# A pre-norm attention and low-rank-expert kernel: another order of loads and matmuls in its prologue

## The reference

```
n = layernorm(x); q, k, v = split(n @ Wqkv.T + bqkv)      # 16 heads of 64
scores = q k^T * 64**-0.5 + q . rel_k[clip(i - j, -64, 64)]
scores below the 32nd largest of their row -> -inf; attn = softmax(scores)
v1 = attn v + attn . rel_v[clip(i - j)];  v2 = attn v1;  v3 = attn v2
x = x + (sum_i sigmoid(alpha_i) v_i) @ Wout.T + bout
x = x + layernorm(x) @ base_w.T + base_b + 2 * (8 experts of rank 8, gated by a softmax)
```

## Time and profile before

| what | value |
|---|---|
| median of 3 runs | 720.5 us (716.99 to 725.43) |
| the profiled execution | 719.82 us, its span 718.1 us |
| mean granted clock of TensorE | 0.982 |
| VectorE busy | 684.0 us (95%) |
| TensorE busy | 658.3 us (92%), weight loads 513.4 us |
| ScalarE busy | 620.5 us (86%) |
| GpSimd busy | 533.5 us (74%) |
| start of the first search | 19.79 us |

### The profile page before, as it was taken

How to read it: one execution, slowest core, us unless ns; L and a number is a source line. 1 busy time by engine, 2 the same in 40 slices (tenths; PEclk the granted TensorE clock), 3 DMA queues, 4 the chain that set the end, 5 groups by cost and what they waited for, 6 DMA issues and landing times.

```text
span 718.1 us, 20880 instructions
## 1 busy us (share of the span) xinstructions
PE 658.3 (92%) x5768; PEld 513.4 (72%) x5768; DVE 684.0 (95%) x2841; ACT 620.5 (86%) x1754; POOL 533.5 (74%) x934
## 2 busy tenths in 40 slices
PE   4378999999999999999999999999999999998795
PEld 3266777777777777777777777777777777776574
DVE  6899999999999999999999999999999999999925
ACT  4588999989999899989999899989999899988833
POOL 1588898778777777877787778777878787877411
PEclk9779999999999999999999999999999999999998
DMA  6735455444544455444545454545454445454202
GB/s 204 189 106 160 128 152 154 144 149 141 151 137 148 138 147 150 136 141 144 150 134 151 133 149 137 154 130 149 137 158 140 138 134 160 129 149 116 63 13 58
DMA packets 148338, 98.72 MB, mean 137 GB/s; under 512 B 10624, under 2 KB 147968, under 8 KB 148096
## 3 DMA queue, kind: packets, MB, share of 16 engines
q1 hardware_dynamic: 147920, 97.32, 46.4%
q10 hardware_dynamic: 304, 0.08, 0.1%
HBM read 45.59 MB, written 51.77 MB: 136 GB/s over the span
## 4 chain that ended last, share of the span: by engine, by line
DVE 79%; issue 9%; PE 6%; POOL 2%; DMA 2%; ACT 1%; SPq 0%; DVEq 0%; ACTq 0%; POOLq 0%
DVE top L666 40%; DVE work L672 35%; DMA band_scratch<-zeros 1%; POOL s_sb L322 1%; DVE rinv L653 1%; PE ps_p L885 1%; PE ps_y L902 1%; PE ps_d L871 1%; PE ps_s L965 1%; ACT a_sb L435 1%; DVE stats L688 0%; PE ps_a L800 0%; DMA band_scratch<-band 0%; DMA skew<-band_scratch 0%; DVE x_sb L681 0%
## 5 line engine op out<-in xcount | busy, mean ns | idle before, releaser
L666 DVE MAX8 top<-work 128x8 f32<-128x256 f32 x768 | 285.0, 414 | 0.0
L672 DVE MATCH_REPLACE8 work<-top,work 128x256 f32<-128x256 f32 x512 | 206.1, 411 | 0.0
L322 POOL TENSOR_TENSOR s_sb<-s_sb,pen 128x512 f32<-128x512 f32 x127 | 162.1, 1276 | 55.0 <-ACT pen L425 54.6
L327 POOL TENSOR_SCALAR a_sb<-a_sb,rinv 128x256 f32<-128x256 f32 x254 | 119.6, 482 | 54.6 <-DVE rinv L653 53.7
L435 ACT ACTIVATE a_sb<-s_sb,nmax 128x256 f32<-128x256 f32 x256 | 128.1, 501 | 34.1 <-POOL s_sb L322 26.2
L425 ACT ACTIVATE pen<-s_sb,limit 128x256 f32<-128x256 f32 x254 | 116.5, 512 | 21.7 <-POOL limit L309 21.7
L297 POOL TENSOR_TENSOR s_sb<-s_sb,skew 128x384 f32<-128x384 f32 x128 | 128.6, 1004 | 3.0 <-DMA skew<-band_scratch 3.0
L885 PE MATMUL ps_p<-aT,rows 128*64 128x256 f32 x1024 | 125.1, 385 | 0.9 <-issue 0.5
L672 DVE MATCH_REPLACE8 work<-top,s_sb 128x256 f32<-128x256 f32 x256 | 103.0, 411 | 0.0
L666 DVE MAX8 top<-s_sb 128x8 f32<-128x256 f32 x256 | 94.5, 411 | 3.5 <-POOL s_sb L297 3.5
L885 PEld LDWEIGHTS ps_p<-aT,rows 128*64 128x64 f32 x1024 | 69.0, 136 | 38.5 <-issue 11.9
(11 more groups left out here) (136 smaller groups left out, 1289.9 us busy)
## 6 DMA issues: line engine op xcount, KB each, us to landing
skew<-band_scratch SPq DMA_DIRECT2D x128, 192.0 KB, 2.8
diag_scratch<-a_sb SPq DMA_DIRECT2D x128, 192.0 KB, 2.2
band_scratch<-band SPq DMA_DIRECT2D x128, 191.0 KB, 3.3
diag<-diag_scratch SPq DMA_DIRECT2D x128, 128.0 KB, 2.2
wqkv<-in_wqkv SPq DMA_DIRECT2D x1, 1152.0 KB, 7.7
x_sb<-in_x SPq DMA_DIRECT2D x4, 256.0 KB, 4.9
wout<-in_wout SPq DMA_DIRECT2D x1, 512.0 KB, 5.7
out<-xn SPq DMA_DIRECT2D x1, 512.0 KB, 3.3
```

The lines of the kernel that those rows point to most:

```text
L322: nc.gpsimd.tensor_tensor(s_sb[g % 4][:], s_sb[g % 4][:], pen[g % 2][:], ALU.subtract).then_inc(pen_added, 1)
L327: nc.gpsimd.tensor_scalar(a_sb[g % 3][:, t, :], a_sb[g % 3][:, t, :], rinv[g % 2][:, t:t + 1], 1.0, ALU.mult, ALU.mult).then_inc(normed, 1)
L666: nc.vector.max(m[:, t, 8 * n:8 * n + 8], src).then_inc(top_step, 1)
L672: nc.vector.match_replace(work[t][:, n % 2, :], m[:, t, 8 * n:8 * n + 8], src, LOW).then_inc(top_step, 1)
```

## The change

x is loaded in five groups, the first two of two tiles each, so that the first sequence stands alone; all statistics, roots, transposes and copies follow these groups (XGROUPS), and the fifth group is transposed at the end of slot 3. TensorE runs 12 products of the ones tile with itself into ps_d before anything else. After q/k(0) and relative(0) come scores(0), then q/k(1), relative(1), q/k(2), and ScalarE saves in the same order, with the second root behind save_scores(0). Pair 0's band is filled and sent head by head (fill_first). SP waits for two of POOL's preparations instead of all, and issues the weights of pairs 2 to 7 after both heads' bands of pair 0.

```diff
--- before.py
+++ after.py
@@ -131,7 +131,7 @@
         ps_z = [ps_qk, ps_a, ps_d]
         ps_l = [ps_s0, ps_s1, ps_qk, ps_a, ps_p0, ps_p1]
 
-        x_in = [sem(f"x_in{g}") for g in range(TILES // 4)]
+        x_in = [sem(f"x_in{g}") for g in range(TILES // 4 + 1)]
         relk_in, cols_in, w_in, w_in2, late_in, wout_in, ffn_in = (
             sem(n) for n in ("relk_in", "cols_in", "w_in", "w_in2", "late_in", "wout_in", "ffn_in"))
         made, scratch_zero = sem("made"), sem("scratch_zero")
@@ -185,17 +185,15 @@
         SLOTS = range(-3, PAIRS + 4)
         MADE = 1 + 1 + 1 + 4 + 1 + 1 + 1
         DONE = TILES - T
-        GROUPS = TILES // 4
+        XGROUPS = [(0, T), (T, 4)] + [(a, a + 4) for a in range(4, TILES, 4)]
 
         @block.sync
         def _(sp):
-            for g in range(GROUPS):
-                sp.dma_start(x_sb[:, 4 * g:4 * g + 4, :], x_d[2 * g:2 * g + 2].rearrange("b (t p) d -> p (b t) d", p=P)
-                             ).then_inc(x_in[g], 16)
+            for g, (a, e) in enumerate(XGROUPS):
+                sp.dma_start(x_sb[:, a:e, :], x_d[a // T:e // T].rearrange("b (t p) d -> p (b t) d", p=P)).then_inc(x_in[g], 16)
                 if g == 0:
                     sp.dma_start(wqkv[:, 0:2, :], wqkv_d[:, 0:2 * 3 * P].rearrange("p (h c) -> p h c", h=2)).then_inc(w_in, 16)
-            sp.dma_start(wqkv[:, 2:NP, :], wqkv_d[:, 2 * 3 * P:].rearrange("p (h c) -> p h c", h=NP - 2)).then_inc(w_in2, 16)
-            sp.wait_ge(made, MADE)
+            sp.wait_ge(made, 2)
             for i in range(2):
                 dst = bass.AP(band_d[i].tensor, DYN, [[2 * ROW, P], [ROW, 2], [1, P]])
                 sp.dma_start(dst, zeros[:, 0:2 * P].rearrange("p (h c) -> p h c", h=2)).then_inc(scratch_zero, 16)
@@ -251,7 +249,7 @@
                 if on(q + 2):
                     p = q + 2
                     for h in range(2):
-                        sp.wait_ge(band_filled, p + 1)
+                        sp.wait_ge(band_filled, p + 2 if p else h + 1)
                         ring(sp, skew_in, 2 * p + h - 4)
                         dst = bass.AP(band_d[p % 2].tensor, h * ROW, [[2 * ROW, P], [DYN + P, T], [1, DYN]])
                         sp.dma_start(dst, band[p % 2][:, h, :].rearrange("p (t c) -> p t c", t=T)
@@ -262,6 +260,9 @@
 
             for q in SLOTS:
                 slot(q)
+                if q == -2:
+                    sp.dma_start(wqkv[:, 2:NP, :], wqkv_d[:, 2 * 3 * P:].rearrange("p (h c) -> p h c", h=NP - 2)
+                                 ).then_inc(w_in2, 16)
                 if q == -1:
                     load_wout()
                 if q == 2:
@@ -309,6 +310,13 @@
                 nc.gpsimd.tensor_scalar(limit[g % 2][:], top8[g % 2][:, :, TOPK - 1], STEEP, 1.0, ALU.mult,
                                         ALU.mult).then_inc(limit_done, 1)
 
+            def fill_first(h):
+
+                pool.wait_ge(band_saved, h + 1)
+                edges = bass.AP(band[0][:].tensor, h * T * DYN + FILL, [[2 * T * DYN, P], [2 * P - 1, 2], [0, FILL]])
+                beyond = bass.AP(band[0][:].tensor, h * T * DYN, [[2 * T * DYN, P], [FILL + 2 * P, 2], [1, FILL]])
+                nc.gpsimd.tensor_scalar(beyond, edges, 1.0, 1.0, ALU.mult, ALU.mult).then_inc(band_filled, 1)
+
             def fill_band(p):
 
 
@@ -352,7 +360,10 @@
                     negative_max(2 * q)
                 if on(q - 1):
                     add_penalty(2 * q - 1)
-                if on(q + 2):
+                if q == -2:
+                    fill_first(0)
+                    fill_first(1)
+                elif on(q + 2):
                     fill_band(q + 2)
                 if on(q):
                     add_skew(2 * q + 1)
@@ -405,11 +416,12 @@
                                         (bqkv[:], bqkv_d.rearrange("p (h c) -> p h c", h=NP), cols_in)):
                 act.dma_start(dst, src).then_inc(semaphore, 16)
             act.wait_ge(var_done, 1)
-            nc.scalar.activation(std[:, 0:4], mv[:, 0:4, 1], ACT.Sqrt).then_inc(std_done, 1)
+            nc.scalar.activation(std[:, 0:T], mv[:, 0:T, 1], ACT.Sqrt).then_inc(std_done, 1)
 
             def save_xnT(g):
                 act.wait_ge(xnT_ready, g + 1)
-                nc.scalar.copy(xnT[:, g * 4 * P:(g + 1) * 4 * P], ps_y[:]).then_inc(xnT_saved, 1)
+                a, e = XGROUPS[g]
+                nc.scalar.copy(xnT[:, a * P:e * P], ps_y[:, 0:(e - a) * P]).then_inc(xnT_saved, 1)
 
             def save_aT(g):
                 p = g // 2
@@ -549,19 +561,19 @@
             save_xnT(0)
             act.wait_ge(cols_done, 1)
             save_queries(0)
+            save_band(0)
+            save_scores(0)
             act.wait_ge(var_done, 2)
-            nc.scalar.activation(std[:, 4:TILES], mv[:, 4:TILES, 1], ACT.Sqrt).then_inc(std_done, 1)
-            for q in (-2, -1):
-                save_band(q + 2)
-                if on(q + 1):
-                    save_scores(q + 1)
-                save_queries(q + 3)
+            nc.scalar.activation(std[:, T:TILES], mv[:, T:TILES, 1], ACT.Sqrt).then_inc(std_done, 1)
+            save_queries(1)
+            save_band(1)
+            save_queries(2)
             act.wait_ge(late_in, 16 * 8)
             nc.scalar.activation(al[:], al[:], ACT.Exp, scale=-1.0).then_inc(alpha_exp, 1)
             act.wait_ge(relv_done, 2 * T + 1)
             for q in range(0, PAIRS):
                 slot(q)
-                if 0 <= q < GROUPS - 1:
+                if 0 <= q < len(XGROUPS) - 1:
                     save_xnT(q + 1)
                 if q == PAIRS - 2:
                     act.wait_ge(y_stats, 1)
@@ -613,8 +625,9 @@
 
             def moments(a, e):
                 for i in range(a, e):
-                    if i % 4 == 0:
-                        dve.wait_ge(x_in[i // 4], 16)
+                    for g, (first, _) in enumerate(XGROUPS):
+                        if i == first:
+                            dve.wait_ge(x_in[g], 16)
                     nc.vector.bn_stats(stats[:, i, :], x_sb[:, i, :]).then_inc(row_stats, 1)
                 for i in range(a, e):
                     dve.wait_ge(row_stats, a + i + 1)
@@ -628,17 +641,17 @@
                     nc.vector.tensor_scalar(xn[:, i, :], x_sb[:, i, :], mv[:, i, 0:1], rstd[:, i:i + 1],
                                             ALU.subtract, ALU.mult).then_inc(xn_done, 1)
 
-            moments(0, 4)
+            moments(0, T)
             dve.wait_ge(std_done, 1)
-            normal_rows(0, 4)
+            normal_rows(0, T)
             dve.wait_ge(relk_in, 32)
             own(nc.vector.tensor_scalar(relkt[:, 0, :], relk[:, 0:P], relk[:, P:VOCAB], None, ALU.subtract))
             nc.vector.tensor_scalar(relkt[:, 1, :], relk[:, 1:VOCAB], relk[:, 0:1], None, ALU.subtract).then_inc(relk_done, 1)
             dve.wait_ge(cols_in, 16)
             nc.vector.tensor_scalar(kcol[:], bqkv[:, :, 1], SCALE, None, ALU.mult).then_inc(cols_done, 1)
-            moments(4, TILES)
+            moments(T, TILES)
             dve.wait_ge(std_done, 2)
-            normal_rows(4, TILES)
+            normal_rows(T, TILES)
             dve.wait_ge(late_in, 16 * 8)
             for t in range(T):
                 nc.vector.tensor_scalar(rcol[:, :, t], bqkv[:, :, 2], relvc[:, t:t + 1], None, ALU.add).then_inc(relv_done, 1)
@@ -786,10 +799,11 @@
             mm, transpose = nc.tensor.matmul, nc.tensor.transpose
 
             def normal_columns(g):
-                pe.wait_ge(xn_done, 4 * (g + 1))
+                a, e = XGROUPS[g]
+                pe.wait_ge(xn_done, e)
                 reach(pe, xnT_saved, g)
-                for i in range(4):
-                    last = transpose(ps_y[:, i * P:(i + 1) * P], xn[:, 4 * g + i, :], ident[:])
+                for i in range(a, e):
+                    last = transpose(ps_y[:, (i - a) * P:(i - a + 1) * P], xn[:, i, :], ident[:])
                 last.then_inc(xnT_ready, 1)
 
             def attention_columns(g):
@@ -803,7 +817,7 @@
 
             def queries_and_keys(p):
                 b, hp = divmod(p, NP)
-                pe.wait_ge(xnT_saved, b // 2 + 1)
+                pe.wait_ge(xnT_saved, [g for g, (a, e) in enumerate(XGROUPS) if a <= T * b][-1] + 1)
                 if p == 0:
                     pe.wait_ge(w_in, 16)
                 ps_k = ps_a[:, 0:N] if p == 0 else ps_qk[:, N:2 * N]
@@ -982,18 +996,21 @@
                         if b == e - 1:
                             last.then_inc(l_ready, 1)
 
+            pe.wait_ge(made, 1)
+            for i in range(12):
+                mm(ps_d[:, 0:P], ones[:], ones[:], start=True, stop=True)
             pe.wait_ge(made, MADE)
             normal_columns(0)
             queries_and_keys(0)
-            for q in (-2, -1):
-                relative_keys(q + 2)
-                if on(q + 1):
-                    scores(q + 1)
-                queries_and_keys(q + 3)
+            relative_keys(0)
+            scores(0)
+            queries_and_keys(1)
```

(4 more changed lines are left out.)

## The result

The changed kernel takes 722.15 us (median of 22 runs, 719.13 to 727.42), the kernel before 718.76 us (22 runs beside it, 716.03 to 725.43). The ratio is 1.0048, 95% interval 1.0032 to 1.0064: slower by half a per cent, 3.4 us, where 1.1 us of gain was forecast. The profiled execution has a span of 722.3 us against 718.1.

A forecast was written before the change was run, and what follows sets the result against it. VectorE's 128 top-32 searches, end to end, bound the kernel. An earlier first search (1.4 us) less later slots (0.3) gave 1.1 us; 719.0 us was put between 718.7 (from the profiled execution) and 719.4 (from the median); range 715.8 to 723.3.

The forecast's parts named there:

- rival C: Ramp: weights arrive late for pair 2, delaying the second search through add_skew(1); 720.4 to 723.3 us; chance 0.30.
- C's upper case: Weights land at 19.7, first search 1.5 us late, second 3.2 us late at the slow clock.
- Two tiles first, warm TensorE, band ready: Prologue: two tiles first save 1.5 us, warm-up 0.2, filling by halves 0.3; band ready at 11.1 instead of 13.12.
- The zero fill: SyncE's queue: without the weights in front, the scratch's zeros land 2.8 us earlier, at 10.9 instead of 13.66.
- When the band lands: Pair 0's bands land 2.55 us (first head) and 3.0 us (second head) after the band leaves.
- T: Time the first band leaves: latest of 10.14, 10.9 and 11.1, about 11.0 instead of 13.68.
- When the weights land: Load behind pair 0's bands: its bytes need 2.8 us, so it lands at 16.8.
- The skew read behind the weights: Pair 0's skew read waits for the weights, lands at 17.3; first search at 18.4, gain 1.4 us.
- The work behind the weights: Chain queries(2) to add_skew(1), 6.74 us: ends at 23.5, just before the second search at 23.8, if TensorE is fast.
- point of decision: Weights' landing from which the second search comes later than before: 18.45 at the fast clock, 16.45 at the slow one.
- the slow clock: TensorE idling before the weights land may fall to 1.2 GHz, adding 2.0 us to pair 2's chain; left open.
- The fifth group in slot 3: Four transposes and a copy in slot 3, where TensorE has no gap: cost 0 to 0.55 us, taken 0.3.

The follow-up runs named there:

- e4: The changed kernel without the 12 products of ones at its start; 720.49 us, ratio 1.0037 to the kernel before.
- e9: The changed kernel with the eight small loads issued by GpSimd, on another queue than SyncE's; 721.83 us, ratio 1.0031 to the kernel before.
- e10: e6 with small loads on GpSimd's queue, wout and second scratch's zero fills in slot 0, 12 more products behind queries(2); 719.07 us, ratio 1.0.
- e6: The changed kernel with weights of pairs 2 and 3 before the zero fills, pairs 4 to 7 behind pair 0's skew reads; 718.38 us, ratio 1.0002.
- e2: The kernel before with only the weights of pairs 2 to 7 moved, issued after both bands of pair 0; 723.29 us, ratio 1.0062.
- e5: The changed kernel with the weights of pairs 2 to 7 issued after pair 0's two skew reads; 726.6 us, ratio 1.0115 to the kernel before.
- e16: The changed kernel with x in four groups again; 722.07 us, ratio 1.0042 to the kernel before.
- e3: The changed kernel with 28 more products of ones between relative(1) and queries(2); 719.79 us, ratio 1.0021 to the kernel before.
- e14: The kernel before with only x in five groups, two tiles first, the fifth transposed at the end of slot 3; 718.59 us, ratio 0.9996.
- e1: The changed kernel with the weights of pairs 2 to 7 back behind the x loads, before the zero fills; 720.04 us, ratio 1.002 to the kernel before.
- e7: e1 with x again in four groups of four tiles; 718.82 us, ratio 1.0007 to the kernel before.
- e13: The kernel before with only the 12 products of ones in front; 717.0 us, ratio 0.9978.
- e15: The kernel before with only scores(0) before queries(1) and the second root behind save_scores(0); 718.08 us, ratio 0.9989.
- e8: The kernel before with weights of pairs 2 and 3 in the old place, pairs 4 to 7 behind pair 0's skew reads; 716.75 us, ratio 0.9992.

## Why the prediction was wrong

Forecast was 719.0, 1.1 us of gain; the kernel lost 3.4. The sum counted only the first search and put the second at no loss; that rested on the weights landing at 16.8 and on a fast TensorE, and both failed (18.7, and the lower clock). The mechanism that decided stood in the text as rival C, at 0.30, and the measured 722.15 lies in its 720.4 to 723.3. That the total fits is in part luck: C's upper case had the weights at 19.7 and the second search 3.2 us late; they came at 18.7 and 2.1 us late, and the rest of the 3.4 us is from elsewhere. The steps:

- **Two tiles first, warm TensorE, band ready.** Right in sum, too careful in the parts: the band is ready at 9.64 (9.06 + 0.58), not 11.1. The warm-up passes took 4.73 us and ended at 5.78, after both rows of xn were there (4.42 + 0.60 = 5.02), so they held up the transposes by 0.45 us (5.62 against 5.17 in e4); in all they made the band ready 0.9 us sooner (9.64 against 10.58), where 0.2 was forecast. e4 shows no difference to the time that is clear of the intervals.
- **The zero fill.** Right: landed 10.35, forecast 10.9.
- **When the band lands.** Failed. I took T + 2.55 from the earlier trace rows as if it held for any T. But in the kernel before too the small loads were in front of the band: VectorE gets the last of them only at 15.32 (the row below), 1.6 us after the band was issued and 0.9 before it landed (16.23). In the changed kernel they are issued only 0.2 us sooner; the last lands near 14.6 and the band at 15.79. So of the 3.3 us by which the band left earlier, 0.4 were left at its landing. With the small loads on another queue the band takes 3.44 us instead of 5.43 (e9), though in e10 it lands no earlier than in e6.

```profile
15.32 0.23 DVE L644 TENSOR_SCALAR rcol<-bqkv,relvc 128x8 f32<-128x8 f32 x1 [0.32 <-DMA al<-in_alphas]
```

- **When the weights land.** The step that failed most: "the weights' bytes behind them need 2.8, landing at T + 5.8 = 16.8". Measured 18.7. I priced the bytes at the 418 GB/s of the earlier trace rows and put the 7.7 us of the earlier trace rows down to the x loads in front. But from issue to landing this load takes 7.4 us in the changed kernel, 6.5 in e2, 6.8 in e9, 7.3 in e4, 7.4 in e5, 7.7 in e16 and 8.8 in e3, with different loads in front. In the changed kernel alone one could lay the miss on the band, since the weights land 2.9 us behind it (15.79 to 18.7), as the 2.8 wanted; e9 speaks against that: its band lands at 14.33 and its weights at 18.6 all the same. The row nearest to the new case was its own one. Why the load takes that long is not shown.
- **The skew read behind the weights.** Right in kind (3.64 us here, 4.90 in e9, 2.46 in e5 where the weights are behind it), and so the rule of the Trainium skill's page "DMA: Bandwidth & Descriptors", section "Queues, rings and completion order", holds against interleaving: the trace agrees, with these three numbers; in the six profiles with the weights in front (changed kernel, e2, e3, e4, e9, e16) the skew read lands 0.6 to 1.4 us after them. The first search at 20.56 against 18.4 is the weights' 1.9 us and 0.25 us more behind them (0.75 instead of 0.5).
- **The work behind the weights.** The chain and its point of decision were right: 18.45 at the fast clock, and the weights landed at 18.7. I priced the slow clock at 2.0 us and left open whether it comes, which was worth more than the gain forecast; it cost 1.7 here (8.45 against 6.74), and with the whole load in a late place and TensorE idle for it the projections of pair 2 took 1.19 us each time (the changed kernel, e2, e4, e5, e9, e16), but 0.67 in e3, where TensorE had the products of ones to do. At the fast clock the chain would have ended at 18.83 + 6.74 = 25.6, and the second search, behind the first, could have started near 26.0 (20.56 + 5.40), 0.8 us late instead of 2.1: an estimate from these rows.
- **The fifth group in slot 3.** Forecast 0.3. e14 (0.9996) and e16 against the changed kernel (1.0042 and 1.0048) show nothing that can be told from zero; a cost of this size stays possible.

**What stays open.** The two searches account for 2.1 us of the 3.4. The rest comes after them. In the profile some of it is in the tail: TensorE's clock is low there for 6.8 us between 673 and 682 us, and for 3.4 us between 671 and 676 us in the kernel before:

```profile
673.00:682.00 9.00, 7.39 (x46) 6.45 (x47) 7.49 (x27) 5.14 (x16) 4.45 (x9) 0.62 0.16 49
```

```profile
671.00:676.00 5.00, 4.62 (x32) 3.90 (x33) 4.33 (x20) 3.19 (x12) 2.03 (x4) 0.66 0.22 66
```

(The first is of the kernel after, the second of the one before; columns as in the earlier trace rows.) But e1 and e7, with the same 3.4 as before, and e4 and e9, whose profiles show none there at all, don't order themselves by it, and single profiles of kernels that time alike have spans from 716.9 (e4) to 722.3. The profiles of e4 and e9, with the second search as late as in the changed kernel (27.22), have rinv waits of 1.9 and 2.0 us in all, less than the 3.4 of the kernel before, and spans of 716.9 and 717.4, below its 718.1. So a late second search does not always bring the later waits. Whether it makes them likelier, or each execution draws them, one profile each does not tell. e1's remaining 0.2% is open too: the parts alone show no cost, and e7 halves it within the noise.

No version beats both kernels for certain. The lowest ratios are those of e13 (0.9978), e15 (0.9989) and e8 (0.9992); of these only the interval of e13 leaves out 1.

## What to carry to other kernels

A wait that sets the pace also covers what stands behind it in the same queue: before moving a load out of its way, ask which loads will then be in front of the transfer that is released, and take the landing time from a row in which the queue is as full, after looking up when the loads in front of it landed. A load moved out of the critical path has a new first user, and everything queued behind that user's wait on each engine (here ScalarE's saves, GpSimd's fill of the next band, and through it VectorE's second search) has to be dated from the landing, measured from issue, not from bytes over bandwidth. Splitting the load, so that the first users get their part early, took the loss away as far as could be measured.

## What the runs showed of the hardware

With the eight small loads, 141 KB in all, in front of it in SyncE's queue, the band took 5.43 us to land, while the DMA engines stood at a share of 0.09 and 20 GB/s from 9 to 12 us; with them on GpSimd's queue it took 3.44 (e9), and the zero fills beside them 0.5 us more. The same 1,152 KB took 6.5 to 8.0 us from issue to landing in all kernels that load them at once, and 8.8 in e3. TensorE's clock fell from 1.00 to 0.50 in the changed kernel near 15.1, with its last matmul ended at 12.2, and at the lower level the same eight relative-key matmuls took 1.23 us against 0.71. With 24 passes of ones from 1.05 on, TensorE ran at the upper level by its first transposes at 5.62 (0.38 us for two, 0.66 without the passes); without them (e4) two projections at 6.28 and 11.15 still took 1.22 us each.
